# A graph layer on one core: edge one-hots compared in f16 a block ahead and widened by ScalarE, halves of the sums added by VectorE, the normalised rows kept in the gathered buffers

## What is computed

```
h    = relu(layernorm(x))                                # 6250 x 96
m    = h[src] + edge_attr                                # 206250 x 96
aggr = segment_sum(m, dst, num_segments=6250)            # 6250 x 96
out  = x + (1 + eps) * h + relu(aggr @ W1 + b1) @ W2 + b2
```

## Time and profile before

| | |
|---|---|
| median of the runs | 561.38 us (560.37 to 562.74, 3 runs) |
| profiled execution, own time | 559.85 us |
| its span, first to last instruction | 558.0 us |
| TensorE busy | 499.2 us, 89% |
| VectorE busy | 504.6 us, 90% |
| ScalarE busy | 375.2 us, 67% |
| GpSimd busy | 353.9 us, 63% |
| granted TensorE clock, mean | 0.988 |
| bytes moved | 120.57 MB, 216 GB/s in the mean |

### The profile page before, as it was taken

The page is one execution under the profiler, slowest core; times in us unless marked ns, Lnnn a source line. Parts: engine busy times, 40 slices in busy tenths (PEclk is TensorE's granted clock), DMA queues, the critical chain, the costliest instruction groups (busy, mean ns, idle before and its releaser), DMA issues.

```text
span 558.0 us, 23440 instructions
## 1 busy us (share of the span) xinstructions
PE 499.2 (89%) x9695; PEld 474.5 (85%) x9695; DVE 504.6 (90%) x676; ACT 375.2 (67%) x613; POOL 353.9 (63%) x200
## 2 busy tenths in 40 slices
PE   0406798999999999999999999999999999999995
PEld 0305788999999999999999999998998999999994
DVE  7989997999999999899998998998998989999840
ACT  0486556677777757776875677677776776775771
POOL 1400048888888888888888887687686478870000
PEclk9999879999999999999999999999999999999998
DMA  6789849999879888999888889988878687985000
GB/s 196 244 283 286 245 122 318 277 307 271 234 196 234 230 210 207 290 262 236 230 232 215 210 217 266 285 215 224 227 206 223 158 241 179 236 226 172 6 11 18
DMA packets 99109, 120.57 MB, mean 216 GB/s; under 512 B 71160, under 2 KB 72792, under 8 KB 98870
## 3 DMA queue, kind: packets, MB, share of 16 engines
q1 hardware_dynamic: 74854, 108.13, 63.3%
q0 software_dynamic: 24144, 10.89, 15.5%
HBM read 112.50 MB, written 6.48 MB: 213 GB/s over the span
## 4 chain that ended last, share of the span: by engine, by line
PE 76%; SPq 7%; ACT 4%; issue 4%; DVE 3%; DMA 3%; POOL 2%; ACTq 0%; DVEq 0%; POOLq 0%
PE agg_ps L973 27%; PE oct_ps L961 21%; PE agg_ps L967 14%; PE key_ps L986 5%; PE mlp_ps L991 4%; SPq L340 3%; ACT adj L810 3%; POOL gathered_edges L477 2%; PE key_ps L978 2%; PE key_ps L979 2%; SPq L339 1%; SPq L341 1%; DMA win<-packed_keys,row_i 1%; ACT hid L826 1%; DVE lo_hot L547 1%
## 5 line engine op out<-in xcount | busy, mean ns | idle before, releaser
L810 ACT ACTIVATE adj<-oct_ps 128x784 f16<-128x784 f32 x360 | 300.6, 867 | 146.9 <-PE oct_ps L961 141.5
L477 POOL DMA_INDIRECT gathered_edges<-h_rows,gather_src x160 | 317.8, 1986 | 97.6 <-DMA gathered_edges<-in_edge_attr 49.1
L973 PE MATMUL agg_ps<-hl,adj 128*128 128x192 f16 x2205 | 227.7, 247 | 0.9 <-issue 0.8
L547 DVE TENSOR_TENSOR lo_hot<-iota_z,key 128x2048 f16<-128x2048 f16 x180 | 219.4, 1219 | 0.0
L961 PE MATMUL oct_ps<-z,lo_hot 128*128 128x98 f16 x2880 | 191.5, 209 | 25.3 <-DVE lo_hot L547 21.0
L547 DVE TENSOR_TENSOR z<-z_marks,key 128x1568 f16<-128x1568 f16 x180 | 174.6, 970 | 22.1 <-PE oct_ps L961 21.7
L961 PEld LDWEIGHTS oct_ps<-z,lo_hot 128*128 128x128 f16 x2880 | 162.5, 99 | 33.5 <-issue 13.9
L973 PEld LDWEIGHTS agg_ps<-hl,adj 128*128 128x128 f16 x2205 | 177.1, 98 | 1.9 <-issue 1.4
L967 PE MATMUL agg_ps<-edges,hot 128*32 128x96 f32 x3440 | 81.1, 250 | 0.0
L967 PEld LDWEIGHTS agg_ps<-edges,hot 128*32 128x32 f32 x3440 | 71.8, 111 | 6.4 <-issue 0.3
L674 DVE TENSOR_TENSOR hot<-iota_w,rel 128x1280 f32<-128x1280 f32 x49 | 73.1, 1492 | 1.7
(11 more groups left out here) (126 smaller groups left out, 204.2 us busy)
## 6 DMA issues: line engine op xcount, KB each, us to landing
edges<-in_edge_attr SPq DMA_DIRECT2D x172, 480.0 KB
gathered_edges<-in_edge_attr SPq DMA_DIRECT2D x24, 480.0 KB
dst<-in_dst SPq DMA_DIRECT2D x180, 5.0 KB
gathered_edges<-h_rows,gather_src POOLq DMA_INDIRECT x160
out<-ob SPq DMA_DIRECT2D x45, 48.0 KB
packed_keys<-adj SPq DMA_DIRECT2D x1, 1632.0 KB, 6.3
h_rows<-edges SPq DMA_DIRECT2D x1, 1200.0 KB, 9.2
h_rows<-edges SPq DMA_DIRECT2D x1, 1152.0 KB, 9.2
```

Of the source, the lines that this page charges most:

```text
L477: nc.gpsimd.indirect_dma_start(out=gathered[k][:, g, t, :], out_offset=None, in_=h_dram, in_offset=bass.IndirectOffsetOnAxis(ap=gather_src ...
L547: return nc.vector.tensor_tensor(out.rearrange("p t (w two) -> p t w two", two=2), marks[0:out.shape[0], 0:width].rearrange("p (o w two) - ...
L810: return nc.scalar.activation(adj[k][:, :, 2 * OCT * o:2 * OCT * (o + 1)].rearrange("p h (t q) -> p t h q", q=2), oct_ps[:, o % 2, :].rear ...
L973: last = nc.tensor.matmul(agg_ps[buf][:, 0:2 * C], adj[buf][:, h, :], hl[:, h, :], start=False, stop=(h == NT - 1), skip_group_check=True)
```

## The change

- The f32 comparison of a main block's destinations is replaced: VectorE makes `rel16` (each value twice, f16) and compares in f16 (`hot16`, the form of `one_hots`), for block b + 1 behind chunk 1 of block b; ScalarE copies it to the f32 `hot[b % 2]` (`next_hots`) behind the turned sums, in attached blocks behind octet 4. The gathered blocks still compare in f32, into `hot[1]`.
- The sums' halves are added by VectorE (`join`, a reduce of 192 columns of PSUM to 96) in place of ScalarE's copy; TensorE turns them by one transpose.
- h lies in the gathered buffers. Main blocks 1 and 2 have edge buffers of their own. The residual is made in nine pieces: tiles 40 to 48 first, which frees one gathered buffer, then eight of five tiles, behind blocks 2 to 10.
- The first gathered load follows the load of block 5, the second that of block 14. The attached blocks are 14, 22, 32 and 42. One window is fetched before the gathers and the others once in 25/3 gathers, not in 7.
- Moments, root and norm are in three parts (16, 16, 17 tiles), and ScalarE makes all of h.

```diff
-ATTACHED = (14, 24, 34, 42)
+ATTACHED = (14, 22, 32, 42)
-FETCH_EVERY = 7
-FETCH_FIRST = 5
+FETCH_EVERY = 25
+FETCH_PER = 3
...
+RES_FIRST = 40
+RES_ROWS = 5
...
-        hot = [sb(f"hot{k}", [P, GROUPS * GT, GROUP]) for k in range(3)]
+        hot = [sb(f"hot{k}", [P, GROUPS * GT, GROUP]) for k in range(2)]
+        hot16 = sb("hot16", [P, GROUPS * GT, GROUP], F16)
+        rel16 = sb("rel16", [P, GROUPS, GT, 2], F16)
...
-        h_sb = edge_home[:, 1:3, :, :, :]...
+        h_sb = gather_home[:, :, :, :, :]...
...
+        THIRDS = [slice(0, 16), slice(16, 32), slice(32, NT)]
+        RES = [(RES_FIRST, NT)] + [(t, t + RES_ROWS) for t in range(0, RES_FIRST, RES_ROWS)]
...
# SyncE
             for b in range(TURN, NM):
                 sp.wait_ge(edges_done, b - TURN + 1)
-                if b == TURN + 1:
-                    load_gathered(0)
-                    sp.wait_ge(res_ready, 2)
-                    sp.wait_ge(h_stored, 32)
                 load(b)
                 if b == TURN + 2:
+                    sp.wait_ge(h_stored, 32)
+                    sp.wait_ge(res_ready, 1)
+                    load_gathered(0)
+                if b == TURN + 2 + len(RES):
+                    sp.wait_ge(res_ready, len(RES))
                     load_gathered(1)
...
# GpSimd
-            fetched = WINS
+            fetched = WINS + 1
+            fetch(WINS)
             pool.wait_ge(h_stored, 32)
...
-                        if (j * GROUPS + g) * GT + t >= (fetched - WINS) * FETCH_EVERY + FETCH_FIRST and fetched < MPAIRS:
+                        if ((j * GROUPS + g) * GT + t) * FETCH_PER >= (fetched - WINS - 1) * FETCH_EVERY and fetched < MPAIRS:
...
# VectorE
             def edge_hots(b):
                 v.wait_ge(ids_in[b % TURN], (b // TURN + 1) * (16 * GROUPS))
-                if b >= 2:
-                    v.wait_ge(edges_done, b - 1)
-                relative(dst_sb[b % TURN], slice(b * GROUPS, (b + 1) * GROUPS), b % 2, rel_ready, b + 1)
-                compare(b % 2).then_inc(hot_ready, 1)
+                if b >= 1:
+                    v.wait_ge(hot_ready, b)
+                nc.vector.tensor_tensor(rel16[:, :, :, :],
+                                        dst_sb[b % TURN][:, :, :].rearrange("p g (t o) -> p g t o", o=1).broadcast_to([P, GROUPS, GT, 2]),
+                                        gbase[:, b * GROUPS:(b + 1) * GROUPS].rearrange("p (g o q) -> p g o q", o=1, q=1).broadcast_to([P, GROUPS, GT, 2]),
+                                        ALU.subtract).then_inc(rel_ready, 1)
+                v.wait_ge(rel_ready, b + 1)
+                one_hots(hot16[:, :, :], rel16[:, :, :, :].rearrange("p g t two -> p (g t) two"), iota_z, GROUPS * GT, GROUP).then_inc(narrow_ready, 1)
...
+            def join(k):
+                return nc.vector.tensor_reduce(agg[:, :], agg_ps[k][:, 0:2 * C].rearrange("p (two c) -> p c two", two=2), AX_X, ALU.add)
+
+            def next_join(n):
+                v.wait_ge(agg_done, n + 1)
+                if n >= 1:
+                    v.wait_ge(aggT_done, n)
+                join(n % 2).then_inc(sums_ready, 1)
...
                 chunk(b, 1)
+                if 2 <= b < NM - 1:
+                    edge_hots(b + 1)
+                if attached(b) is not None:
+                    gathered_hots(attached(b))
                 if b >= 4:
                     finish(b - 4)
                 if attached(b - 3) is not None:
                     finish_gathered(attached(b - 3))
+                if b >= 2:
+                    next_join(b - 2)
                 if b == 1:
                     low_part(1)
                 for c in range(2, CHUNKS):
                     chunk(b, c)
-                if b in (1, 2):
-                    residual(b - 1)
+                    if b + c == CHUNKS - 1:
+                        edge_hots(b + 1)
+                if 2 <= b < 2 + len(RES):
+                    residual(b - 2)
...
# ScalarE
+            def next_hots(b):
+                act.wait_ge(narrow_ready, b + 1)
+                if b >= 2:
+                    act.wait_ge(edges_done, b - 1)
+                if attached(b - 1) is not None:
+                    act.wait_ge(gather_summed, attached(b - 1) + 1)
+                nc.scalar.activation(hot[b % 2][:, :, :], hot16[:, :, :], ACT.Copy).then_inc(hot_ready, 1)
+
+            next_hots(0)
             for b in range(NM):
                 here, behind = attached(b), attached(b - 1)
-                if b >= 2:
-                    next_sums(b - 2)
...
                             next_turned(b - 2)
+                        if b + 1 < NM and here is None:
+                            next_hots(b + 1)
...
                             take_gathered_sums(b % 2).then_inc(gather_agg_read, 1)
+                            next_hots(b + 1)
...
# TensorE
-            def turn_both():
-                nc.tensor.matmul(key_ps[0:C, TURN_AT:TURN_AT + P], agg[:, 0:C], ident[:, :], start=True, stop=False)
-                return nc.tensor.matmul(key_ps[0:C, TURN_AT:TURN_AT + P], agg[:, C:2 * C], ident[:, :], start=False, stop=True)
+            def turn_sums():
+                return nc.tensor.transpose(key_ps[0:C, TURN_AT:TURN_AT + P], agg[:, :], ident[:, :])
```

More of the change, by code:

```diff
@@ L309, in edge_rows @@
         def edge_rows(b):
-            return gathered[b % 2] if b in (1, 2) else edges[b % TURN]
+            return edges[b % TURN]
         block = ctx.enter_context(nc.Block())
@@ L598, in _ @@
             v.wait_ge(x_in[0], 16)
-            moments(0, HALF // 2)
+            chain(moments(0, 16))
+            variance(0)
             v.wait_ge(cnt_done, 1)
@@ L615, in _ @@
             nc.vector.tensor_scalar(e_tab[:, :], e_raw[:, :], float(ELAST), None, ALU.min).then_inc(tab_ready, 1)
-            nc.vector.tensor_copy(span[:, :], oct_ps[0:1, 0, 0:GCOLS])
-            nc.vector.tensor_copy(ends[:, :], oct_ps[0:1, 0, 512:512 + GCOLS])
             nc.vector.tensor_copy(reach_row[:, :], key_ps[0:1, 2 * P:3 * P]).then_inc(spread_read, 1)
-            normal(0)
+            chain(moments(26, 32))
+            variance(1)
             def pick(q):
@@ L625, in pick @@
                 nc.vector.tensor_scalar(keyT[q % 2][:, :], win[q % WINS][:, :, 0], base[:, q:q + 1], 1.0 / SPREAD, ALU.subtract, ALU.mult).then_inc(keys_ready, 1)
-            v.wait_ge(x_in[1], 32)
-            chain(moments(HALF, NT))
             pick(0)
-            variance(1)
             normal(1)
-            v.wait_ge(norm_ready, 2)
-            for t in range(HALF, NT):
-                last = nc.vector.tensor_scalar(h_sb[:, t, :], x_sb[:, t, :], rstd[:, t:t + 1], shift[:, t:t + 1], ALU.mult, ALU.add)
-            last.then_inc(scaled_ready, 1)
+            nc.vector.tensor_copy(span[:, :], oct_ps[0:1, 0, 0:GCOLS])
+            nc.vector.tensor_copy(ends[:, :], oct_ps[0:1, 0, 512:512 + GCOLS]).then_inc(spread_read, 1)
+            chain(moments(32, NT))
+            variance(2)
+            normal(2)
             def passes_needed():
-                v.wait_ge(spread_read, 1)
+                v.wait_ge(spread_read, 2)
                 nc.vector.tensor_scalar(row[:, :], row[:, :], keep[:, 0:1], None, ALU.mult)
@@ L716, in _ @@
                 v.wait_ge(key_read, b // 2 + 1)
-                edge_hots(b)
-                if attached(b) is not None:
-                    gathered_hots(attached(b))
+                if b == 0:
+                    edge_hots(0)
                 if b == 0:
@@ L741, in _ @@
                 finish_gathered(attached(NM - 3))
-            for b in range(NM - 3, NM):
-                finish(b)
+            next_join(NM - 2)
+            finish(NM - 3)
+            finish(NM - 2)
+            next_join(NM - 1)
+            finish(NM - 1)
             v.wait_ge(need_ready, 1)
@@ L843, in _ @@
             deviation(0)
[L844 to L846 removed]
+            act.wait_ge(falls_clear, 1)
+            act.wait_ge(steps_ready, 1)
+            nc.scalar.activation(steps.bitcast(F32), steps, ACT.Relu, scale=-1.0, accum_out=falls[:, 0:1]).then_inc(falls_ready, 1)
+            for t in range(NT):
+                for k in range(1, 3):
+                    if t == THIRDS[k].start:
+                        deviation(k)
+                for k in range(3):
+                    if t == THIRDS[k].start:
+                        act.wait_ge(norm_ready, k + 1)
+                last = nc.scalar.activation(h_sb[:, t, :], x_sb[:, t, :], ACT.Relu, bias=shift[:, t:t + 1], scale=rstd[:, t:t + 1])
+                if t + 1 == HALF:
+                    last.then_inc(h_ready, 1)
+                if t + 1 == KEYS_AFTER:
                     next_keys(0)
[L848 to L850 removed]
+                if t + 1 == HALF:
+                    high_part(0)
             last.then_inc(h_ready, 1)
[L852 to L854 removed]
             high_part(1)
             act.wait_ge(w_in, 16 * 5)
[L858 to L862 removed]
             def next_turned(n):
@@ L1007, in next_turn @@
                     pe.wait_ge(hid_ready, n)
```

(4 more changed lines are left out.)

74 lines of the change are left out of this document (29 added, 45 removed).

## The result

The changed kernel takes 553.28 us (median of 4 runs, 552.01 to 555.09), the kernel before 560.88 beside it (559.35 to 562.74): a ratio of 0.9884, 95% interval [0.985, 0.9919] (the quotient of the two medians is 0.9864), so a little faster. The forecast was 552.4 us. The profiled execution is the slowest of the four, 555.09 us with a span of 553.3; the forecast span was 549.0. A second comparison later, on another chip, gave 0.9958 [0.9916, 1.0] (557.58 against 560.37 us, 10 and 25 runs). So the gain is some 0.4 to 1.2%, and the second interval reaches up to no gain.

The account below looks back on a forecast made before the run. TensorE was taken to set the pace, VectorE close behind. Block 22's edges at 285.0, plus 261.3 to the end and a 2.7 wait, gave 549.0 us of span; with 1.85 and 1.53 added, 552.4 us, range 545 to 563.

Parts of the forecast that it names:

- TensorE's turn: Each block: one transpose replaces four matmuls, saving 0.335 us; period 10.16 us, 14.7 us over 44 blocks.
- VectorE's price list: VectorE's instructions per block: 9.6 us, 0.2 more in every second block, under 10.16; VectorE bounds in blocks 3 to 10.
- Rival (d): VectorE each block: join costs far more than its row, 1.2 us; 565.7 us; chance 0.05.
- ScalarE's copy: The widening copy takes 1.2 us, free in plain blocks, showing in four attached blocks; 4.6 us.
- The start: Blocks 0 to 4: early delays recovered, block 4's edges begin at 96.3 instead of 99.44, 3.1 us won.
- The gathers: Second forty, block 22: first gather at 96, ready at 289.4, wanted at 286.7; a wait of 2.7 us.
- window fetches between them: Fetches on GpSimd between the first 80 gathers: ten at 1.63 us, 16.3 us.
- the disputed term: Pace of a gather on GpSimd: 2.17 us taken, bounds 2.05 and the old 2.29.
- The sum: Whole span: block 22's edges at 285.0, 261.3 from there to the end, 2.7 of wait; 549.0 us.
- the forecast case: Block 22 waits 0 to 6 us for gathered rows; 549.7 to 555.7 us; chance 0.40.

Follow-up runs that it names:

- gathered_load_first: The changed kernel with the first gathered load issued ahead of block 5's load; ratio 0.9957 to the kernel before, on the slower chip.
- copy_after_octet_7: The changed kernel with ScalarE's copy in attached blocks moved from behind octet 4's read to behind octet 7's; 554.37 us, ratio 0.9855.
- split_compare: The kernel before with its f32 comparison in two instructions of half the size; 560.92 us, ratio 1.0015.
- turn_undone: The changed kernel with ScalarE's copy of 192 columns and the two accumulated products back, no join; ratio 1.0062, on the slower chip.
- late_and_early_reads_again: The changed kernel with attached blocks 16, 26, 34, 42, their copy behind octet 7, and block 0's octets 0 and 1 read before the copy; 544.96 us, 0.9725.
- f32_compare: The changed kernel with the f32 comparison on VectorE at the new place and no copy on ScalarE; 556.17 us, ratio 0.9901.
- join_and_window: The kernel before with VectorE's join, the single transpose and one window fetched ahead of the gathers; ratio 0.9818 on the slower chip, 0.9886 when repeated.
- join_alone: The kernel before with VectorE's join and the single transpose, nothing else; 554.59 us, ratio 0.9895.

## Why the prediction came out as it did

**TensorE's turn: right.** One transpose of 0.13 us, a period of 10.16 us.

**VectorE's price list: right.** 0.82 for the compare (forecast 0.82), 0.24 for `rel16` (0.25), 0.355 for `join` (0.35); the next instruction starts 0.27 us after `join`. The eight residual pieces cost about 0.63 (0.65). Rival (d), a dear `join`, is out. What I didn't see is that `join` stands behind `rel16` in VectorE's order, so that late destinations reach TensorE: 1.51 us in block 14, and 4.72 in `gathered_load_first`.

**ScalarE's copy: right in size and place.** 1.28 us, free in plain blocks and 1.28 at octet 7 of each attached block. The prediction counted 1.2 for each; the timeline of the kernel before names no wait at that place, so all of it is new. Taking it away (`copy_after_octet_7`) moved the total by nothing that can be told.

**The start: too pessimistic by 2.6 us.** Block 4's edges at 93.66, not 96.3. Octet 2 started at 48.78, not at 51: I had put h's end at 46.5 and it was 44.55. Block 2's edges ended at 74.8, not at 77.5, and the prediction's own addends for that point, 75.92 + 2.16, make 78.1. They follow a stretch in which the kernel before ran at a granted clock of 0.83 (55 to 65 us) and 0.74 (65 to 75 us), TensorE being busy 8.9 and 6.4 us of the ten; the changed kernel had 1.00 in both, and its edges of block 2 take 1.86 us, not 2.16. That too the prediction left out.

**The gathers: right in mechanism, mis-sized.** This is the step that failed in its terms. Forecast: ready at 96.2 + 80 x 2.17 + 10 x 1.63 + 3.3 = 289.4. Measured: 293.9, and the place of the error can be read off.

| term | forecast | measured |
|---|---|---|
| first gather | 96.2 | 96.5 |
| 80 gathers | 173.6 (2.17) | 174.9 (2.186: 2.228 in the first forty, 2.146 in the second) |
| window fetches between them | 16.3 | 19.4 |
| to landing | 3.3 | 3.2 |
| ready | 289.4 | about 294 |
| wanted | 286.7 | 287.4 |

The pace, which the prediction called the disputed term, was off by 0.016 us. The fetches, which it took for settled at 1.63 each, cost more: two of the nine between these gathers (I had counted ten; the first now stands before the first gather) took 3.97 us each. The wait is 6.57 us where 2.7 was forecast, just past the upper end of 0 to 6 that it gave. For the first forty the prediction said ready near 195 for 200.7: issued at 195.00, it landed at 201.4, because four fetches took 11.6 us where I had counted 8.2 for five, and the last gather landed 6.38 us after its start.

**The sum.** Against the forecast span of 549.0: the start 2.6 less; block 4 to 14 takes 104.2 for 102.6 (the turn's 1.51 in block 14); 14 to 22 takes 87.7 for 86.1 (the 1.79 for gathered rows); the gap is 3.9 longer; the rest 0.2 less, although the gathered sum at the lower clock put 1.4 on it, so that something else in it came 1.6 cheaper, which I have not traced. That is -2.6 + 1.6 + 1.6 + 3.9 - 0.2 = +4.3, which is 553.3. The median lies only 0.9 above the forecast because the profiled run was this time the slowest, 1.8 above its median, while I had taken the profile of before as 1.5 below. The step from the kernel's profile to the median was 3.3 us of luck against 4.3 us of error. The mechanisms of the forecast case hold; the agreement of the medians is closer than the sum earned, and the second comparison, 0.9958, puts it in its place.

**What sets the pace of a gather.** The trace of before led me to its borders with VectorE's instructions, and I gave the shorter compare the credit. `split_compare` speaks against that: same length as the f16 form, same pace as before. What goes with the pace is how much VectorE does beside it. Over the stretch of the gathers VectorE is busy 84% of the time in `turn_undone`, and a gather takes 1.82 us; 91% in the changed kernel, 1.84 and 1.86; 94% in `late_and_early_reads_again`, 1.88; 95% in `f32_compare`, 1.93; and 94 to 97% in the kernels with the f32 compare in the order of before, 1.96 to 2.01. Beside an idle VectorE it is 1.55, as at 294.54 and 296.39 in the gap of the changed kernel. The share does not order all of them: at 94% it is 1.88 with the f16 pair and 1.99 in the kernel before, and `gathered_load_first` has 1.87 at 88%. Which of VectorE's instructions costs a gather how much stays open. The Trainium skill ("SBUF — State Buffer", SBUF: two separate sides) has GpSimd wait for the whole of a two-input instruction of VectorE. That gathers are faster beside an idle VectorE agrees with it; that halving such an instruction changed nothing speaks against taking its length alone for the price.

**Where the gain is.** By the runs: the join with one transpose is worth about 1% alone (0.9895), as much as the change (0.9884 and 0.9958), and the change without it is worth nothing (1.0062, on the second chip). The f16 pair gives VectorE 0.65 us a block, but its gain was spent: the order that came with it moved the first gather from 77.4 to 96.5 us, and the attached blocks two earlier, into a wait of 6.6 to 7.5 us. With the attached blocks moved back (0.9787) and the start's reads drawn ahead (0.9725 and 0.975) the gain shows. How much of these last is the f16 pair's, and how much would be had with an f32 compare at the same places, no run tells apart.

**Left open.** Why the second chip is slower: there, in `turn_undone` and `join_and_window`, TensorE's sums of edges take and wait some 12 to 15 us more (in `join_and_window` 89.9 us of busy time for the 81.1 of `join_alone`, the same 3440 products, and 3.6 us of "issue" before them), which would fit late edge rows, but no run tested it. And TensorE has single waits of 0.8 to 1.4 us that the profile calls "issue" in the kernels on all chips (1.35 at 206.73 in `join_alone`); I did not find what they are.

## What to carry to other kernels

When a change shortens the blocks and also delays a slow side stream (here GpSimd's gathers), write down for each consumer when it is ready and when it is wanted, and move the consumer, not only the stream: two and four blocks later was worth 5.5 us here, as much as the join and the single transpose by themselves (5.3). Price the clock with the wait: a wait of 6.6 us left the sum behind it at a lower clock and cost 1.4 more. In such a sum the terms that look settled need the same care as the disputed one; the pace was right to 1%, the fetches between were 19% off. And before crediting a speed-up to one edit of several, run that edit alone: here the join with its single transpose gained by itself as much as the whole change.

## What the runs showed of the hardware that was not expected

A GpSimd window fetch that takes 1.0 to 1.6 us in the other places took 3.97 us in two, each time started in the same `lo_hot` of VectorE's order and ended just behind the start of `finish`, the first of two instructions that read PSUM. The timeline of the changed kernel:

```profile
119.34 1.22 DVE L553 TENSOR_TENSOR lo_hot<-iota_z,key 128x2048 f16<-128x2048 f16 x1
119.64 3.97 POOL L454 DMA_INDIRECT win<-packed_keys,row_i  x1 [0.30 <-issue]
...
122.76 0.82 DVE L553 TENSOR_TENSOR hot<-iota_z,rel 128x1280 f16<-128x1280 f16 x1
123.50 0.25 DVE L711 TENSOR_TENSOR ob<-x_sb,mlp_ps 128x96 f32<-128x96 f32 x1
123.67 0.35 DVE L721 TENSOR_REDUCE agg<-agg_ps 128x96 f32<-128x192 f32 x1
```

It ends at 123.61, 0.11 behind the start of `finish` and past four borders of VectorE's work; the one at 160.66 ends 0.10 us behind the start of `finish` there. A gather of 4.49 us from 99.18 spans the same sequence, `finish` and `join` too, and ends 0.24 us behind the start of the next `z`. So GpSimd does not step on at every border, as I had read the trace of before: all five instructions beside which the fetches stood take two inputs from SBUF, and `finish` takes one from PSUM. The Trainium skill ("SBUF — State Buffer", SBUF: two separate sides) counts instructions with two SBUF inputs among those that hold the port pair shared with GpSimd, against a GpSimd instruction that reads SBUF; these two rows agree with it. But they do not show that it takes a PSUM operand to let GpSimd on. The kernel before has a long gather too, and its timeline is:

```profile
202.41 4.01 POOL L477 DMA_INDIRECT gathered_edges<-h_rows,gather_src  x1 [0.30 <-issue]
...
205.04 1.49 DVE L674 TENSOR_TENSOR hot<-iota_w,rel 128x1280 f32<-128x1280 f32 x1
...
206.45 0.97 DVE L547 TENSOR_TENSOR z<-z_marks,key 128x1568 f16<-128x1568 f16 x1
```

It ends at 206.42, ahead of a `z` with two SBUF inputs, and no instruction that reads PSUM stands near. The four gathers of 4.45 to 5.02 us in `f32_compare` and the three of 4.82 in `join_alone` end the same way, 1.36 to 1.42 us behind the start of the f32 compare, which is where it ends. In `split_compare` one of 4.01 us from 121.19 ends at 125.20, 1.38 behind the start of the first half, so it passed the border between the halves as well. What nearly all the long ones share is that they end with the compare of the edges, f16 or f32. Why there, and why most gathers get through sooner, no run tested.
